# Four PSUM regions for the bias rows of a batch, and transposes that no longer wait for their addition

## What is computed

```python
# cross attention, per batch
sim   = (ctx @ Wq.T) @ (ctx @ Wk.T).T * scale          # 512 x 512, the heads are summed
keep  = sim >= (153rd largest of its row)
A     = sigmoid(sim) * keep
x    += (1 - g) * layernorm(x) + g * 0.5 * (A + A.T)   # g = sigmoid(gamma_raw)
# mixture of 16 experts, 4 for each of the 2048 tokens
xn    = layernorm(x)
s     = softmax over the 4 largest of (xn @ Wr.T + br), 0 elsewhere
for e in range(16):
    gate, up = split(xn @ gate_up[e] + gate_up_bias[e])
    h  = (clip(up, -7, 7) + 1) * min(gate, 7) * sigmoid(1.702 * min(gate, 7))
    x += s[:, e] * (h @ down[e] + down_bias[e])
```

## Time and profile before

| | us |
|---|---|
| median of 3 runs | 970.09 |
| lowest and highest | 966.62, 971.19 |
| the profiled execution | 970.89 |
| its span, first to last instruction | 969.2 |
| TensorE busy in it | 777.6 |
| VectorE busy | 617.8 |
| ScalarE busy | 398.8 |
| GpSimd busy | 343.0 |

### The profile page before, as it was taken

The page is one execution under the profiler, slowest core; times in us unless marked ns, Lnnn a source line. Parts: engine busy times, 40 slices in busy tenths (PEclk is TensorE's granted clock), DMA queues, the critical chain, the costliest instruction groups (busy, mean ns, idle before and its releaser), DMA issues.

```text
span 969.2 us, 16996 instructions
## 1 busy us (share of the span) xinstructions
PE 777.6 (80%) x3556; PEld 626.2 (65%) x3557; DVE 617.8 (64%) x1082; ACT 398.8 (41%) x659; POOL 343.0 (35%) x383
## 2 busy tenths in 40 slices
PE   4354462544179999999999999999999999999980
PEld 2024241424058888887888887887788878888870
DVE  3786787674737575577666676577667576775540
ACT  3957749232024242334524344344433244342220
POOL 1522484852613233233332332333333233232220
PEclk9565565555579999999999999999999999999995
DMA  8301130813115455376574655656666354732335
GB/s 278 134 0 44 44 44 2 173 48 105 44 45 166 97 140 125 65 203 181 114 190 108 169 165 133 176 172 163 186 165 175 89 129 135 218 64 47 65 54 184
DMA packets 70128, 117.32 MB, mean 121 GB/s; under 512 B 28672, under 2 KB 30976, under 8 KB 69952
## 3 DMA queue, kind: packets, MB, share of 16 engines
q1 hardware_dynamic: 30368, 77.62, 24.0%
q0 software_dynamic: 18336, 38.35, 20.7%
q10 hardware_dynamic: 21312, 0.16, 1.3%
HBM read 87.98 MB, written 32.31 MB: 124 GB/s over the span
## 4 chain that ended last, share of the span: by engine, by line
PE 67%; DVE 11%; ACT 6%; issue 5%; POOL 2%; DMA 2%; another core or an unknown queue 2%; SPq 1%; DVEq 1%; ACTq 0%; POOLq 0%
PE gate_up_ps L784 37%; PE bank L784 19%; ACT junk L486 3%; PE bank L766 3%; PE bank L774 3%; POOL slot_rows L360 2%; PE gate_up_ps L688 2%; PE gate_up_ps L717 1%; DVE A L966 1%; PE gate_up_ps L731 1%; DMA bd_raw<-_ffn_down_proj_bias_dram 1%; DVE w L1187 1%; DVE gu L1162 1%; DVE x_sb L971 1%
## 5 line engine op out<-in xcount | busy, mean ns | idle before, releaser
L784 PE MATMUL gate_up_ps<-w,xh 128*128 x1152 | 363.3, 397 | 1.7 <-DVE xl L1151 1.7
L411 POOL DMA_INDIRECT acc_rows<-yb,aslot x72 | 128.5, 1785 | 439.9 <-ACT yb L603 434.7
L784 PEld LDWEIGHTS gate_up_ps<-w,xh 128*128 128x128 f32 x1152 | 211.7, 189 | 42.8 <-issue 2.1
L784 PE MATMUL gate_up_ps<-w,xl 128*128 x576 | 226.1, 392 | 0.0
L784 PE MATMUL bank<-w,hh 128*128 x576 | 180.6, 395 | 8.5 <-DVE hl L1156 8.2
L596 ACT ACTIVATE sg<-gc 128x512 f32<-128x512 f32 x72 | 45.6, 634 | 214.5 <-DVE gc L1166 214.5
L1162 DVE TENSOR_TENSOR gu<-gate_up_ps,bgu 128x1024 f32<-128x1024 f32 x72 | 88.1, 1224 | 70.4 <-PE gate_up_ps L784 69.6
L784 PEld LDWEIGHTS bank<-w,hh 128*128 128x128 f32 x576 | 107.8, 189 | 37.0 <-issue 15.4
L1156 DVE TENSOR_TENSOR hl<-bank,hh 128x512 fp32r<-128x512 f32 x72 | 49.5, 688 | 120.3 <-ACT hh L590 120.3
L784 PEld LDWEIGHTS gate_up_ps<-w,xl 128*128 128x128 f32 x576 | 108.5, 188 | 23.5
L1187 DVE TENSOR_TENSOR w<-raw_w,w 128x1536 f32 x60 | 103.2, 1760 | 28.6 <-issue 19.7
(11 more groups left out here) (198 smaller groups left out, 819.2 us busy)
## 6 DMA issues: line engine op xcount, KB each, us to landing
raw_w<-_L_ffn_gate_up_proj_dram SPq DMA_DIRECT2D x64, 512.0 KB
raw_w<-in_L_ffn_down_proj_dram SPq DMA_DIRECT2D x64, 256.0 KB
bgu<-n_gate_up_proj_bias_dram SPq DMA_DIRECT2D x16, 512.0 KB
x_sb<-in_x_dram SPq DMA_DIRECT2D x4, 1024.0 KB, 11.4
xn_rows<-xn SPq DMA_DIRECT2D x4, 1024.0 KB
acc_rows<-xn SPq DMA_DIRECT2D x4, 1024.0 KB
gslot<-slot_rows ACTq DMA_DIRECT2D x75, 1.0 KB
xg<-xn_rows,gslot POOLq DMA_INDIRECT x74, 4.9
```

The lines of the kernel that those rows point to most:

```text
L411: pool.indirect_dma_start(acc_d, bass.IndirectOffsetOnAxis(aslot[:, k, 0:1], 0), yb[:, k % 2, :], None, compute_op=ALU.add).then_inc(S["ad ...
L784: last = nc.tensor.matmul(out_ps, lhs[:, rows], w[:, bass.ds(buf, 1), part, c, cols].rearrange("p a d -> p (a d)"), start=(m == 0), stop=( ...
```

## The change

It gives each bias product of a batch a region of its own: the two banks of the scores, the first half of `psG[1]`, and its second half, where the router's results and ranks lie (for the last batch `bank0` in its place, since counts are still read from there). The waits are placed anew:

- The bias products wait no more for additions. They wait for the scores that lie in their banks to be copied out, `s_done` (L751 of the changed kernel).
- The transposes of A wait no more for the additions of the batch before, nor does the count of rows, `count_ok`.
- The scores of batch 3 wait for the additions of batch 0, and the transposes of xn for all additions up to the batch before.
- VectorE waits for its own additions before it writes x1.

```diff
         ps_t = [psG[0][:, 0:512], psG[0][:, 512:1024]]
-        ps_bd = [psG[1][:, 0:512], psG[0][:, 512:1024]]
         ps_m = psG[1][:, 512:1024]
...
-        ps_ok = ps_bd[0][:, 0:RT]
+        ps_ok = psG[1][:, 0:RT]
+        ps_bd = [[bank67[0][:], bank67[1][:], psG[1][:, 0:512], ps_m if b < NB - 1 else banks[0][:]] for b in range(NB)]
...
             def scores(b):
                 pe.wait_ge(S["qk_done"], 2 * b + 2)
+                if b >= 3:
+                    pe.wait_ge(S["bo_done"], RT * (b - 2))
...
                 pe.wait_ge(S["ok_done"], b + 1)
-                if b >= 2:
-                    pe.wait_ge(S["bo_done"], RT * (b - 1))
                 nc.tensor.matmul(ps_ok, ones[:], okv[:], start=True, stop=True).then_inc(S["ok_ps"], 1)
...
                 pe.wait_ge(S["a_done"], RT * (b + 1))
                 if b:
                     pe.wait_ge(S["scT_done"], b)
-                if b:
-                    pe.wait_ge(S["bo_done"], RT * b)
...
                 if b:
 
                     pe.wait_ge(S["payload_done"], b)
+                    pe.wait_ge(S["bo_done"], RT * b)
...
-                for r in range(RT):
-                    i = RT * b + r
-                    if i >= 2:
-                        pe.wait_ge(S["bo_done"], i - 1)
-                    nc.tensor.matmul(ps_bd[r % 2], denseT[:, r * P:(r + 1) * P], bd_sb[:], start=True, stop=True).then_inc(S["bd_ps"], 1)
+                pe.wait_ge(S["s_done"], RT * min(b + 3, NB))
+                for r in range(RT):
+                    nc.tensor.matmul(ps_bd[b][r], denseT[:, r * P:(r + 1) * P], bd_sb[:], start=True, stop=True).then_inc(S["bd_ps"], 1)
...
-                V.tensor_tensor(base_out[:, r, :], ps_bd[r % 2], x1[:, r, :], ALU.add).then_inc(S["bo_done"], 1)
+                V.tensor_tensor(base_out[:, r, :], ps_bd[b][r], x1[:, r, :], ALU.add).then_inc(S["bo_done"], 1)
...
                     dve.wait_ge(S["xn2_done"], RT * b)
+                    dve.wait_ge(S["bo_done"], RT * b)
```

## The result

The changed kernel takes 962.87 us, median of 6 runs (961.0 to 963.68). The kernel before, 6 runs on the same chip, takes 967.12 us (966.61 to 971.19). The medians differ by 4.3 us. The ratio, which is taken of the means, is 0.9942 with a 95% interval of 0.9921 to 0.9963: 5.6 us faster, 3.6 to 7.6. The forecast was 963.1 us, which the median meets to 0.2 us, and that it gets faster is clear of the noise. Whether by over 0.5% is not: the ratio says 0.58%, the medians 0.44%, and the interval begins at 0.37%. The forecast's base, 970.09 us, was the median of three runs, and with six it is 3 us lower. So a gain of 7.0 us was forecast, and 4.3 (medians) or 5.6 us (ratio) measured. The profiled execution took 962.98 us, against 970.89 before.

What follows compares the result with a forecast made beforehand. The prediction took a chain through four batches, before the TensorE-filled expert part, to bound the kernel. Terms 3.4 + 1.8 + 1.8 = 7.0 us off 970.09 gave 963.1 us, range 957.0 to 969.0.

Steps and rivals of the forecast that it cites:

- Iteration 1: Bias products stop waiting for additions, so projection and transposes of A start earlier, limited by ScalarE's search: 3.4 us gained.
- Iterations 2 and 3: Transposes of A run before VectorE's additions end, so x1 of batches 2 and 3 begins earlier: 1.8 us gained each.
- The own wait: VectorE's new wait for its last addition before x1: 0.1 us taken, from a range of 0.0 to 0.36.
- Edits at nothing: Moved waits of bias products, scores of batch 3 and transposes of xn, and the last batch's additions: counted as 0.
- The clock: Idle time before iteration 1's projection could keep TensorE at 1.2 GHz, losing 0.8 us; the clock was taken to rise.
- Sum: Terms of the three iterations, 3.4 + 1.8 + 1.8 = 7.0 us, taken off the 970.09 us median.
- x1 of batch 3 at about 209.2: Sign of being right: VectorE's x1 operations of batch 3 begin at about 209.2 us.
- The expert part has taken it back: Scatters start 7 us earlier but the whole isn't shorter; held excluded by the expert part's clock and TensorE busy share.
- Rival 1: Batch 2: if the end of scatters releases ScalarE's copies of transposed xn, 1.8 us is lost: 964.9 us; chance 0.20.
- Rival 3: Stalls shrink: with the stores of xn elsewhere, one of two stalls goes, 5.9 us more: 957.2 us; chance 0.13.
- Rival 2: Batch 3: store of xn overlapping scatters brings a third stall of 5.9 us: 970.8 us, slower by 0.7; chance 0.12.
- Rival 4: Stands between bias products are held by something else ending at the same time; time stays 970.1 us; chance 0.05.

Runs made afterwards that it cites:

- second pair: The kernel before and the changed kernel, both run again with no edit: 972.82 and 965.01 us.
- split pair: The kernel before and the changed kernel, each with the 16 scatters beside batches 1 and 2 issued as two trains of 8: 965.21 and 959.54 us.
- u23: Changed kernel with the transposes of A of batches 2 and 3 waiting for all additions again: 970.21 us, ratio 0.9977 to the kernel before.
- split_u23: Changed kernel with two trains of 8 scatters, and the transposes of A of batches 2 and 3 waiting for all additions again: 959.8 us, ratio 0.9911.
- nosc: Changed kernel with all 64 scatters issued behind GpSimd's own loop over the batches: 989.23 us in one execution.
- split4: Changed kernel with two trains of 8 scatters and four PSUM regions for the transposes of A in batches 2 and 3: 956.62 us, ratio 0.9839.
- u1: Changed kernel with the projection of batch 3 waiting for the first two additions again: 967.65 us, ratio 0.9949 to the kernel before.
- k_after: Changed kernel run again with no edit: 965.01 us, ratio 0.9918 to the kernel before.
- s_after: Changed kernel with SP storing xn of a batch only when its copies are done: 964.01 us, ratio 0.9915 to the kernel before.
- four: Changed kernel with the later store of xn and four PSUM regions for the transposes of A in batches 2 and 3: 962.46 us, ratio 0.9902.
- split: Changed kernel with the 16 scatters beside batches 1 and 2 issued as two trains of 8, weight conversion between them: 959.54 us, ratio 0.9864.
- k_before: The kernel before, run again with no edit for its trace: 972.82 us, ratio 1.0001.

## Why the prediction was right, and where it wasn't complete

- **Iteration 1, 3.4 us.** Measured 3.37 between the first two traces, 3.3 in the second pair, 3.55 in the split pair, and 3.0 by undoing the wait without the 0.36 us. Each step of the working was found: products in 2.07 us on end, projection at 110.47 (110.4 forecast), context copy at 111.75 (111.76), transposes at 115.93 (116.0), x1 at 117.13 (117.13). ScalarE's search, not the projection's own 3.7 us, was the limit.
- **Iterations 2 and 3, 1.8 us each.** 1.80 and 2.06 in the split pair, 1.68 in the second column of the repeated pair. Undoing gives 1.48 for iteration 2, in u23 and in split_u23; it puts back only the wait ahead of the transposes (1.45 before), not the 0.36 us between the pairs of additions, so it gives less. For iteration 3 undoing gives no clean number: 2.91 us in u23, with a hold in it, and 0.01 in split_u23, with the conversion lying otherwise. Its term rests on the split pair.
- **The own wait, 0.1 us** taken from a range of 0.0 to 0.36 as the gap behind the last addition: 0.09. With the overlap that is lost it is 0.17 us; the sum had the overlap in, since it counted the last addition to its end.
- **Edits at nothing.** The products find the banks of the scores free (idle before them 0.67 us, as before, by the copy of the transposed router scores). The scores of batch 3 begin at 119.09 us behind the transposes, where 119.0 was forecast, and wait for nothing. They cost nothing.
- **The clock.** Its loss did not come: the four scores of batch 3 take 3.68 us again, all at a granted clock of 1.00. The clock stands at the low level, 0.50, from 108 to 116 us in both kernels, so the 0.83 us of idle time ahead of the projection had nothing to bring down. It rises at about 116.9 us after and at about 120.2 before, some 3.3 us earlier like the work itself, which is why the mean of 112 to 126 us went from 0.71 to 0.83. The price of 0.8 us was misread, though. The scores of batch 2 ran at 0.82 on average, at 0.50 only in the first 1.6 of their 4.49 us, and not "for the most part". In the changed kernel the four matmuls of the projection, at 0.50, take 3.79 us (L674 and L675, 112.36 to 116.15), so eight would take some 7.6 us by that pace, an estimate: a clock that stays low would have cost some 3.9 us, not 0.8.
- **Sum, 7.0 us.** 7.65 us at the scatters without holds, 7.8 with them, 5.6 and 8.0 us by the ratios of two comparisons, whose intervals (3.6 to 7.6, 5.3 to 10.6) both hold 7.0. The step that was weak is the base. I took the median of three runs, which was 3.0 us too high for this comparison; with a base of 967.1 the same sum gives 960.1, 2.8 us below what was measured. That the forecast missed by only 0.2 us is luck: the base was 3.0 us too high and the medians fell by 2.8 us less than the sum.
- **A sign was added up wrongly.** "x1 of batch 3 at about 209.2" takes off 5.2 us, without iteration 3's own term. In the trace of before x1 of batch 3 begins at 170.06 + 44.36 = 214.42 us, so by the terms it should come at 207.4. It came at 204.25 in the first trace, 3.2 us earlier, which is the surplus.
- **"The expert part has taken it back" was held to be excluded.** 10.2 us at the scatters became 7.9 in the first pair. The time from the first transposed gather (L766 before) to the end of the span is 700.7 us after and 698.5 before. Over the executions profiled since then it lies between 697.0 and 702.3 us, for kernels that start it anywhere between 255.8 and 289.2 us: 698.4 in nosc, 697.4 in split4, 702.3 in u1. It scatters by itself, and no giving back shows above that.
- **Rival 1** (the gain of batch 2 swallowed, 964.9 us) was right in one half: the scatters do cause the holds. But the gain isn't swallowed. **Rival 3** (a hold goes, 957.2 us) came true in part: in batch 2 the third copy is free in every run with one train of 16 and the change whole in iterations 2 and 3 (after, k_after, u1, s_after, four), though in the last four VectorE's count is held instead. That is worth 1.0 to 1.4 us, not 5.9. The evidence for it was in the trace of before, had I counted from the train's first scatter and not from its last: unheld, the third copy of batch 2 would come 14.3 us after it, and the change brings it to 12.5 us. **Rival 2** did not come as a loss. Its sign shows, though: the third copy of batch 3 waits 3.1 to 3.9 us, where 2.43 is plain, in k_after, u1, s_after, four, split and split4. The fourth copy is on time in all six, so it costs nothing. **Rival 4** did not come.
- **Open.** What inside the chip releases a held wait. In every train of 16 with a hold beside batch 1 or 2, the last held wait ends 1.6 to 2.2 us after the last scatter's issue ends, on ScalarE as on VectorE: in batch 2 of k_after, VectorE's at 190.17, 1.9 us after 187.26 + 0.96 = 188.22. But the third copy of batch 2 of k_before is released while scatters are still issued. Why the first trace of the changed kernel had no hold in batch 1, with its third and fourth copies 15.3 and 17.7 us into the train, the third as far as in k_after, isn't known either. Nor is it known where between 8 scatters and 16 a train becomes long enough: the third copies of batch 2 give 12.5 us in as free and 13.8 us in as held, and nothing was run between.

## What to carry to other kernels

Where an engine stands between two products because another engine must first empty their buffer, look at what is queued behind it on the same engine: here the gain of four buffers wasn't the addition, which stayed where it was, but the projection and the transposes behind it. Price such a change at the first place where the engines meet again (ScalarE's search in iteration 1, VectorE's additions in 2 and 3), not by the length of the stand: 3.2 us of it gave 3.4 and 1.8. And measure a term by itself, between two events of the trace, when single executions scatter by as much as the term; the median of three runs is a poor base for 0.7%.

## What the runs showed of the hardware that I had not expected

- **A long train of small scatters holds other engines' waits.** 16 indirect DMAs issued on end by GpSimd, 1.27 us apart, make waits on ScalarE of 2.4 us stand 4.9 to 9.8 us, all but the shortest with no releaser in the profile, in third copies that are due 13.8 us or more into the train. One due 12.5 us in was never held, and with trains of 8 none was; in one trace copies due 15.3 and 17.7 us in were free as well. VectorE's waits are held too, by 2.8 to 4.2 us for the count of batch 2 in four traces, and up to 9.7 us in nosc, with no pause at all. Cutting the train in two took 7.4 us off the kernel before; by the traces of the changed kernel part of that is not the holds but the moved conversion. The store of xn beside the scatters, which I had suspected, has no part in it.
- **A wait of VectorE for its own last addition leaves 0.09 us behind its end,** 0.17 us more than an operation without such a wait, which starts 0.08 us before that end.
- **GpSimd's cast and subtract of 128x1536 (L386, L388; 4.9 to 5.3 us together) stretch VectorE's operations beside them,** and not all of them: L903 from 0.75 to 3.92 us in split, L1018 from 0.43 to 3.62 in the first trace after; MAX8 keeps its 1.29 us in split_u23.
- **The mean granted clock of a fixed stretch rose because the work moved.** Over 112 to 126 us it was higher than before with TensorE busy 9.92 us instead of 11.93, because the piece of work in which it rises, the transposes of A, came 3.5 us earlier. The pause of 0.83 us ahead of the projection fell into the low level (0.50), so these runs don't show what a pause does to a high clock.
